# Attention over 3,202 keys: the sums of the probabilities folded by adding transfers instead of a product

## The chip, the core and the metric

The kernel runs on one core of a Trainium2 chip. The metric is the device time of one execution in microseconds, lower is better. The engines named below are PE (TensorE), ACT (ScalarE), DVE (VectorE), POOL (GpSimd) and SP (SyncE, which here only issues transfers).

## What is computed

A cross-attention of 4,096 queries over 3,202 keys with 16 heads of 32, a projection and a residual, then a layer of eight experts of which each token takes two. The change touches only the softmax's denominator, the sum over keys.

```python
def _L0_xattn_ref(queries, keys, values, Wq, bq, Wk, bk, Wv, bv, Wo, bo):
    q = (queries @ Wq + bq).reshape(B, L, H, E)
    k = (keys @ Wk + bk).reshape(B, S, H, E)
    v = (values @ Wv + bv).reshape(B, S, H, E)
    scale = 1.0 / sqrt(E)
    scores = jnp.einsum('blhe,bshe->bhls', q, k)
    A = jax.nn.softmax(scale * scores, axis=-1)
    out = jnp.einsum('bhls,bshd->blhd', A, v)
    out = out.transpose(0, 2, 1, 3).reshape(B, L, H * E)
    return out @ Wo + bo
...
    x = x + _L0_xattn_ref(_layernorm(x, axis=-1), ctx_1024, ctx_1024, ...)
    x = x + _L0_ffn_ref(_layernorm(x, axis=-1), ...)
```

## The kernel before

Three stages follow each other: projections of keys, values and queries (to 278 us), the attention (to about 1,935 us), then routing and experts. The change is in the second.

The attention runs in 32 rounds, `it` 0 to 31: four groups of four heads (HG = 4), and in each eight blocks of 512 queries. A round goes through 25 tiles `t` of 128 keys. The 3,202 keys leave two over; they are **the rest**, which is computed for all four heads in one step of its own, on 72 partitions (the same eight rows three times, for high and low parts), at the place REST_TILE of the round.

For each tile PE makes the scores of four heads (12 products of 32 rows, float32 taken as high and low parts), ACT takes the exponential in two instructions, the first head and the other three, into one of P_RING = 9 slots of `probs` (128 keys x 4 heads x 512 queries), and PE weighs the values with it. PE is two tiles ahead with its scores. A slot may be written again, nine tiles on, when PE has weighed it and when it has been added up.

The adding is split. Of 25 tiles DVE adds 21, alternately into `even_sums` (two buffers, by round) and `odd_sums`: 19 adds of 128x2048 in a round, called k = 0 to 18 here; the first two each add two tiles. The tiles PILED = 4, 9, 14, 19 are added by transfers into `pile`, issued by GpSimd: the first a plain copy (`pile_up(it, 0)`), the others adding transfers (`accum_op`), each waiting for the landing of the one before. At the round's end DVE merges `odd_sums` and `pile` into `even_sums` (two instructions, each waiting for the end of its predecessor).

What is left is a sum over the 128 partitions. PE makes it in the next round, at the rest's place: a product of `rest_split` with ones (line 1322) and one of `even_sums` with ones (line 1300), which also spreads the sum over the 32 rows of each head. ACT copies it from PSUM to `recip`; a transfer stores four rows to DRAM, another loads them as 128x16; DVE inverts (INVERT_AT, after add 5), and two more steps store the inverses and broadcast them to `recip`. DVE multiplies the results `o_sb` with them (NORMALISE_AT, after add 9), and SP stores. ACT had fetched the results from PSUM in between the two exponentials of tile 1. The rest's probabilities must be split into a high and a low part before PE can weigh them (tile 21): ACT copies them to `rest_split`, and DVE subtracts, ahead of add 8.

The order on each engine is the order in which the code is written; semaphores with counts join them. Transfers issued by GpSimd run in one queue, those by SP in another. The last round's sums are made by PE after the loop.

## Time and profile before

| | us |
|---|---|
| median of 3 runs | 2379.47 |
| lowest, highest | 2377.31, 2384.11 |
| the profiled execution | 2381.51 |
| its span, first to last instruction | 2379.7 |
| PE, DVE, ACT, POOL busy in the span | 96%, 85%, 78%, 21% |
| granted clock of PE, mean | 0.981 of 2.4 GHz |

The profile is of one execution. A line of a timeline gives start, duration, engine, line of the code, operation, output<-inputs and shape; in brackets how long the engine was idle before it and what ended that. PE, ACT and DVE overlap an instruction's end with the next one's beginning, so pitches (start to start) say what a row of instructions costs, and durations a little more. A product of float32 that the program writes once stands twice in PE's rows.

### The profile page before, as it was taken

What the parts mean: (1) busy time and instruction counts of PE and PEld (TensorE: products, weight loads), DVE (VectorE), ACT (ScalarE), POOL (GpSimd) and SP (SyncE); (2) the same over time, 40 slices, a digit from 0 to 9 for tenths busy, and PEclk for the clock granted to TensorE, in tenths of its full rate; (3) what the DMA queues carried; (4) which work ended last, traced back from release to release, by engine and by line L of the source; (5) the groups of instructions that cost most, each with busy time, mean ns of one, the idle gap of its engine ahead of it and who ended that gap; (6) DMA issues with size and microseconds to landing.
All of it is one profiled execution on the core that took longest, in us unless ns stands there. A gap on an engine that the chain in (4) does not pass through costs nothing. (4 is left out here: it accounts for less than half of the span.)

```text
span 2379.7 us, 49163 instructions
## 1 busy us (share of the span) xinstructions
PE 2275.9 (96%) x19632; PEld 1097.8 (46%) x19632; DVE 2018.2 (85%) x1866; ACT 1855.5 (78%) x2155; POOL 508.8 (21%) x631
## 2 busy tenths in 40 slices
PE   8999699999999999999999999999999999789898
PEld 7878533333333333333333333333333357578786
DVE  4358489999999999999999999999999988867565
ACT  3223299999999999999999999999999956534332
POOL 2213211311111111111111111111111113146664
PEclk9999899999999999999999999999999999889999
DMA  7436564345464455557444434644544467634463
GB/s 267 168 135 213 179 168 108 90 110 114 112 178 108 110 128 134 132 133 199 108 112 112 117 90 128 155 114 108 117 97 101 101 175 266 205 106 141 147 205 120
DMA packets 140924, 333.70 MB, mean 140 GB/s; under 512 B 28918, under 2 KB 61654, under 8 KB 123548
## 3 DMA queue, kind: packets, MB, share of 16 engines
q0 software_dynamic: 43008, 193.75, 33.8%
q1 hardware_dynamic: 95356, 129.20, 16.6%
q10 hardware_dynamic: 2336, 7.60, 0.9%
q8 instruction: 160, 2.62, 0.5%
q14 instruction: 64, 0.52, 0.1%
HBM read 131.16 MB, written 82.78 MB: 90 GB/s over the span
## 5 line engine op out<-in xcount | busy, mean ns | idle before, releaser
L1133 ACT ACTIVATE probs<-psum 128x1536 f32<-128x1536 f32 x800 | 1164.7, 1456 | 0.0
L1300 PE MATMUL psum<-probs,v_st 128*32 128x512 f32 x6400 | 853.2, 605 | 0.2 <-ACT probs L1133 0.2
L1251 PE MATMUL psum<-q_st,k_st 32*128 32x512 f32 x9600 | 779.1, 425 | 43.2 <-ACT probs L1130 27.4
L1251 PEld LDWEIGHTS psum<-q_st,k_st 32*128 32x128 f32 x9600 | 402.2, 183 | 745.5 <-ACT probs L1130 431.0
L1207 DVE TENSOR_TENSOR even_sums<-even_sums,probs 128x2048 f32<-128x2048 f32 x288 | 658.6, 2287 | 75.6 <-ACT probs L1133 74.6
L1207 DVE TENSOR_TENSOR odd_sums<-odd_sums,probs 128x2048 f32<-128x2048 f32 x256 | 588.4, 2299 | 3.1 <-ACT probs L1133 3.1
L1130 ACT ACTIVATE probs<-psum 128x512 f32<-128x512 f32 x800 | 481.0, 601 | 40.1 <-PE psum L1251 32.4
L1300 PEld LDWEIGHTS psum<-probs,v_st 128*32 128x32 f32 x6400 | 126.1, 108 | 289.0 <-issue 278.8
L2087 PE MATMUL psum<-we_hi,wo 128*128 x624 | 219.1, 412 | 7.6 <-ACT wo L1926 4.4
L948 POOL DMA_DIRECT2D pile<-probs x96 | 85.2, 888 | 495.4 <-DMA pile<-probs 308.2
L2087 PEld LDWEIGHTS psum<-we_hi,wo 128*128 128x128 f32 x624 | 119.7, 192 | 34.4 <-issue 8.7
L1919 ACT ACTIVATE shared_rows<-hold 128x512 f32<-128x512 f32 x78 | 63.5, 815 | 91.0 <-DMA hold<-token_rows,whole 49.0
L2087 PE MATMUL psum<-we_lo,wo 128*128 x312 | 125.0, 401 | 0.0
L945 POOL DMA_DIRECT2D pile<-probs x32 | 18.0, 564 | 495.0 <-ACT probs L1133 470.8
L1926 ACT ACTIVATE wo<-psum 128x512 fp32r<-128x512 f32 x78 | 46.3, 593 | 89.3 <-PE psum L2073 73.6
L345 POOL TENSOR_TENSOR squares<-o_hi 128x512 fp32r<-128x512 f32 (+1 forms) x60 | 60.6, 1018 | 207.0 <-ACT o_hi L383 120.1
L763 PE MATMUL psum<-wo,q_st 128*128 128x512 f32 x384 | 96.4, 400 | 0.0
L383 ACT ACTIVATE o_hi<-psum,bk_col 128x512 fp32r<-128x512 f32 (+1 forms) x28 | 17.4, 642 | 91.7 <-PE psum L593 91.7
L1207 DVE TENSOR_TENSOR even_sums<-probs 128x2048 f32<-128x2048 f32 x32 | 73.1, 2285 | 12.6 <-ACT probs L1133 12.6
L1978 DVE TENSOR_TENSOR wo<-psum,wo 128x512 fp32r<-128x512 f32 x78 | 53.9, 691 | 35.2 <-ACT wo L1926 26.9
L763 PEld LDWEIGHTS psum<-wo,q_st 128*128 128x128 f32 x384 | 73.5, 191 | 16.6
L1212 DVE TENSOR_TENSOR even_sums<-even_sums,odd_sums 128x2048 f32<-128x2048 f32 x32 | 74.3, 2322 | 1.1
(229 smaller groups left out, 2262.8 us busy)
## 6 DMA issues: line engine op xcount, KB each, us to landing
pile<-probs POOLq DMA_DIRECT2D x128, 1024.0 KB, 7.5
token_rows<-rows SPq DMA_DIRECT2D x8, 1028.0 KB, 6.7
xn<-in_x SPq DMA_DIRECT2D x16, 512.0 KB, 6.5
qh_scratch<-o_hi SPq DMA_DIRECT2D x8, 1024.0 KB, 4.5
ql_scratch<-o_lo SPq DMA_DIRECT2D x8, 1024.0 KB, 7.5
q_st<-qh_scratch SPq DMA_DIRECT2D x32, 256.0 KB, 4.4
q_st<-ql_scratch SPq DMA_DIRECT2D x32, 256.0 KB, 5.1
token_rows<-in_x SPq DMA_DIRECT2D x8, 1024.0 KB, 7.6
```

The source lines that it names most:

```text
L345: pool.tensor_tensor(squares[:, j, 0:w], h, h, ALU.mult).then_inc(squared, 1)
L763: mm = pe.matmul(psum[:, bank, :], A[:, j, :], W[:, j, :], start=False, stop=t == len(terms) - 1)
L948: pool.dma_start(out=pile[:], in_=probs[:, p_slot(it, t)], accum_op=ALU.add).then_inc(piled, 16)
L1130: act.activation(probs[:, p, 0, :], psum[:, FIRST_BANK, :], ACT.Exp, bias=-WIDEST, scale=SCALE).then_inc(first_done, 1)
L1133: act.activation(probs[:, p, 1:HG, :], psum[:, bank(t, 1):bank(t, 1) + HG - 1, :], ACT.Exp, bias=-WIDEST, scale=SCALE).then_inc(exp_done, 1)
L1207: nc.vector.tensor_tensor(into[:], a, probs[:, p_slot(it, t)], ALU.add).then_inc(added, 1)
L1212: nc.vector.tensor_tensor(total[:], total[:], odd_sums[:], ALU.add).then_inc(added, 1)
L1251: return nc.tensor.matmul(psum[:, bank(t, h), :], k_st[rows, part, t * P:(t + 1) * P], q_st[it % 2][rows, of, :], start=start, stop=stop)
L1300: mm = nc.tensor.matmul(psum[h * DH:(h + 1) * DH, bank, :], lhs(h), rhs(h), start=start, stop=stop)
L1919: act.activation(xs[s % 2], r[:, 0:D], ACT.Identity, bias=r[:, SHIFT_AT:SHIFT_AT + 1], scale=r[:, RSTD_AT:RSTD_AT + 1]).then_inc(xs_done, 1)
L1978: dve.tensor_tensor(x_lo[s % 2], psum[:, T_BANK + s % 2, :].rearrange("p (k n) -> p k n", k=KT), x_hi[s % 2].bitcast(F32), ALU.subtract).t ...
L2087: mm = pe.matmul(psum[:, OUT_BANKS[s % 4], :], A[s % 2][:, k, :], W[:, k, ds(e, 1), :].rearrange("p o n -> p (o n)"), start=t == 0, stop=t ...
```

## The change

REST_TILE moves from 5 to 2: scores and exponential of the rest stand in a round's third place, ahead of tile 2. ACT fetches the results of the round before right ahead of that exponential, no longer inside tile 1. Splitting the rest moves to GpSimd: a `tensor_copy` of 72x512 and a `tensor_tensor` of 8x512.

The sum over partitions is no product any more, but for the last round's. GpSimd issues three adding transfers that fold `even_sums` onto its first 64, 32 and 16 partitions, a store of these 16 rows to DRAM beside the rest's two rows, and four loads that gather the 18 rows of each head as 128 partitions x 18 x 16 (`spread`). DVE reduces over the 18 and inverts, now after add 11, and normalises after add 15. The inverse's round trip through DRAM is as before; GpSimd issues it between the piles of tiles 14 and 19.

```diff
-REST_TILE = 5
+REST_TILE = 2
+FOLDED, REST_KEYS = 16, 2
 PILED = (4, 9, 14, 19)
-REST_LOW_AT, REST_V_AT, REST_AT = 8, 13, 21
-INVERT_AT, NORMALISE_AT = 5, 9
+REST_V_AT, REST_AT = 13, 21
+INVERT_AT, NORMALISE_AT = 11, 15
 WO_AFTER, REST_AFTER = 3, 5
-FETCH_TILE = 1
...
-    spread = sb("spread", [P, CH // DH], F32)
-    spread_inv = sb("spread_inv", [P, CH // DH], F32)
-    sum_d, inv_d = (dram(name, [HG, CH], F32) for name in ("sum_scratch", "inv_scratch"))
+    fold_d = [dram(f"fold_scratch{b}", [FOLDED + REST_KEYS, HG, CH], F32) for b in range(2)]
+    inv_d = dram("inv_scratch", [HG, CH], F32)
     sums_ready = sem("sums_ready")
-    sums_copied = sem("sums_copied")
-    bounced = sem("bounced")
+    sums_moved = sem("sums_moved")
+    rest_stored = sem("rest_stored")
     sums_spread = sem("sums_spread")
...
+MOVES = {P // 2: 0, P // 4: 1, P // 8: 2, "store": 3, "inverse": 4}
+
+
+def moved(it, what):
+
+    return 16 * (it * len(MOVES) + MOVES[what] + 1)
+
+
+def fold_sums(pool, a, it, total, rows):
+    if 2 * rows in MOVES:
+        pool.wait_ge(a["sums_moved"], moved(it, 2 * rows))
+    pool.dma_start(out=total[0:rows], in_=total[rows:2 * rows], accum_op=ALU.add).then_inc(a["sums_moved"], 16)
+
+
+def store_folded(pool, a, it, total):
+    pool.wait_ge(a["sums_moved"], moved(it, FOLDED))
+    pool.dma_start(a["fold_d"][it % 2][0:FOLDED], total[0:FOLDED]).then_inc(a["sums_moved"], 16)
+
+
+def store_rest(pool, a, it, rest_probs, REST, LAST):
+    rows = a["fold_d"][it % 2][FOLDED:].rearrange("x h q -> h x q")
+    for h in range(HG):
+        pool.dma_start(rows[h], rest_probs[h * LAST:(h + 1) * LAST, :]).then_inc(a["rest_stored"], 16)
+
+
 def spread_sums(pool, a, it):
-    pool.wait_ge(a["sums_copied"], it + 1)
-    pool.dma_start(a["sum_d"], a["recip"][0:P:DH, :]).then_inc(a["bounced"], 16)
-    pool.wait_ge(a["bounced"], it * 32 + 16)
-    pool.dma_start(a["spread"][:], a["sum_d"].rearrange("h (p f) -> (h p) f", p=DH)).then_inc(a["sums_spread"], 16)
+    pool.wait_ge(a["sums_moved"], moved(it, "store"))
+    pool.wait_ge(a["rest_stored"], 16 * HG * (it + 1))
+    for h in range(HG):
+        pool.dma_start(a["spread"][h * DH:(h + 1) * DH], a["fold_d"][it % 2][:, h, :].rearrange("r (p f) -> p r f", p=DH)).then_inc(a["sums_spread"], 16)
+
+
+def store_inverses(pool, a, it):
+    pool.wait_ge(a["inverted"], 2 * (it + 1))
+    pool.dma_start(a["inv_d"].rearrange("h (p f) -> (h p) f", p=DH), a["spread_inv"][:]).then_inc(a["sums_moved"], 16)
 
 
 def broadcast_inverses(pool, a, it):
-    pool.wait_ge(a["inverted"], it + 1)
-    pool.dma_start(a["inv_d"].rearrange("h (p f) -> (h p) f", p=DH), a["spread_inv"][:]).then_inc(a["bounced"], 16)
-    pool.wait_ge(a["bounced"], it * 32 + 32)
+    pool.wait_ge(a["sums_moved"], moved(it, "inverse"))
+    if it > 0:
+        pool.wait_ge(a["o_final"], it)
     for h in range(HG):
         pool.dma_start(a["recip"][h * DH:(h + 1) * DH, :], a["inv_d"][h:h + 1, :].to_broadcast([DH, CH])).then_inc(a["inv_in"], 16)
 
 
 def invert_sums(dve, a, it):
-    dve.wait_ge(a["sums_spread"], it * 16 + 16)
-    dve.reciprocal(a["spread_inv"][:], a["spread"][:]).then_inc(a["inverted"], 1)
+    dve.wait_ge(a["sums_spread"], (it + 1) * (16 * HG))
+    dve.tensor_reduce(a["spread_sum"][:], a["spread"][:].rearrange("p r f -> p f r"), AX.X, ALU.add).then_inc(a["inverted"], 1)
+    dve.wait_ge(a["inverted"], 2 * it + 1)
+    dve.reciprocal(a["spread_inv"][:], a["spread_sum"][:]).then_inc(a["inverted"], 1)
 
 
...
+                def split_rest(it):
+                    pool.wait_ge(exp_done, it * STEPS + REST_TILE + 1)
+                    store_rest(pool, results, it, rest_probs, REST, LAST)
+                    if it > 0:
+                        pool.wait_ge(pv_done, (it - 1) * NT + REST_AT + 1)
+                    pool.tensor_copy(rest_split[:], rest_probs[:]).then_inc(rest_high, 1)
+                    pool.wait_ge(rest_high, it + 1)
+                    pool.tensor_tensor(rest_split[DH:DH + REST, :], rest_probs[DH:DH + REST, :],
+                                       rest_split[DH:DH + REST, :].bitcast(F32), ALU.subtract).then_inc(rest_ready, 1)
+                    pool.wait_ge(rest_ready, it + 1)
+
                 for it in range(NIT):
+                    total = even_sums[(it - 1) % 2]
+                    if it > 0:
+                        pool.wait_ge(added, it * adds)
+                        fold_sums(pool, results, it - 1, total, P // 2)
+                    split_rest(it)
                     pile_up(it, 0)
                     if it > 0:
-                        spread_sums(pool, results, it - 1)
-                        broadcast_inverses(pool, results, it - 1)
+                        fold_sums(pool, results, it - 1, total, P // 4)
+                        fold_sums(pool, results, it - 1, total, P // 8)
+                        store_folded(pool, results, it - 1, total)
                     else:
                         pool.wait_ge(wo_hi_ready, 1)
                         pool.tensor_tensor(wo_lo, wo_raw[:], wo_hi.bitcast(F32), ALU.subtract).then_inc(wo_lo_ready, 1)
-                    for i in range(1, len(PILED)):
-                        pile_up(it, i)
+                    pile_up(it, 1)
+                    if it > 0:
+                        spread_sums(pool, results, it - 1)
+                    pile_up(it, 2)
+                    if it > 0:
+                        store_inverses(pool, results, it - 1)
+                        broadcast_inverses(pool, results, it - 1)
+                    pile_up(it, 3)
...
-                def copy_sums(it):
-                    act.wait_ge(sums_ready, it + 1)
-                    if it > 0:
-                        act.wait_ge(o_final, it)
-                    act.activation(recip, psum[:, SUM_BANK, :], ACT.Copy).then_inc(sums_copied, 1)
-
...
                     act.wait_ge(s_ready, it * STEPS + REST_TILE + 1)
                     if it > 0:
                         act.wait_ge(rest_ready, it)
+                        act.wait_ge(rest_stored, 16 * HG * it)
                     act.activation(rest_probs[:], psum[0:REST_ROWS, REST_BANK, :], ACT.Exp, bias=-WIDEST, scale=SCALE).then_inc(exp_done, 1)
-                    act.wait_ge(exp_done, it * STEPS + REST_TILE + 1)
-                    if it > 0:
-                        act.wait_ge(rest_used, it)
-                    act.activation(rest_split[:], rest_probs[:], ACT.Copy).then_inc(rest_high, 1)
...
                         if t == REST_TILE:
+                            if it > 0:
+                                fetch(it - 1)
                             rest(it)
-                            if it > 0:
-                                copy_sums(it - 1)
                         if t == FIRST_HIGH_TILE and it == NIT - 1:
...
-                        if t == FETCH_TILE and it > 0:
-                            fetch(it - 1)
...
                     if k == 0 and it > 1:
-                        dve.wait_ge(sums_ready, it - 1)
+                        dve.wait_ge(sums_moved, moved(it - 2, "store"))
...
-                        if k == REST_LOW_AT:
-                            dve.wait_ge(rest_high, it + 1)
-                            dve.tensor_tensor(rest_split[DH:DH + REST, :], rest_probs[DH:DH + REST, :],
-                                              rest_split[DH:DH + REST, :].bitcast(F32), ALU.subtract).then_inc(rest_ready, 1)
...
                         if t == REST_TILE:
                             rest_scores(it, shifted)
-                            if it > 0:
-                                sum_probs(it - 1, SUM_BANK)
```

The instructions as the program issues them, GpSimd in the second round, before (lines 945 and 948 are the piles; `shared_rows` holds `recip` and the results):

```order
L945 DMA pile<-probs 128x2048
L777 DMA sum_scratch<-shared_rows 4x512
L779 DMA spread<-sum_scratch 128x16
L784 DMA inv_scratch<-spread_inv 128x16
L787 DMA shared_rows<-inv_scratch 32x512 x4
L948 DMA pile<-probs 128x2048 x3
```

and with the change (976 and 979 are the piles now, CAST is the `tensor_copy`):

```order
L785 DMA even_sums<-even_sums 64x2048
L796 DMA fold_scratch<-rest_probs 2x512 x4
L986 CAST rest_split<-rest_probs 72x512
L988 TENSOR_TENSOR rest_split<-rest_probs,rest_split 8x512
L976 DMA pile<-probs 128x2048
L785 DMA even_sums<-even_sums 32x2048
L785 DMA even_sums<-even_sums 16x2048
L790 DMA fold_scratch<-even_sums 16x2048
L979 DMA pile<-probs 128x2048
L803 DMA spread<-fold_scratch 32x18x16 x4
L979 DMA pile<-probs 128x2048
L808 DMA inv_scratch<-spread_inv 128x16
```

The first pile of a round now stands behind a fold, four stores and two computing instructions; the second, third and fourth each behind a part of the sums' way.

PE at the rest's place in the second round, before (in the branch for wide scores, which has the products with `shift_ones` and `rest_shift` in addition; the runs take the other):

```order
L1285 MATMUL psum<-q_st,rest_k 72x512 x3
L1288 MATMUL psum<-q_st,rest_shift 72x512
L1322 MATMUL psum<-rest_split,rest_ones 128x512
L1300 MATMUL psum<-even_sums,ones 32x512 x4
L1251 MATMUL psum<-q_st,k_st 128x512 x12
```

and with the change:

```order
L1340 MATMUL psum<-probs,v_st 32x512 x4
L1325 MATMUL psum<-q_st,rest_k 72x512 x3
L1328 MATMUL psum<-q_st,rest_shift 72x512
L1291 MATMUL psum<-q_st,k_st 128x512 x12
L1315 MATMUL psum<-q_st,shift_ones 128x512 x4
```

The two products of sums are gone, and the scores of the next tile stand right behind the rest's.

## Rows read from the trace of the kernel before

**Rows 1.** The page, part 1: busy us and share of each engine.
```profile
PE 2275.9 (96%) x19632; PEld 1097.8 (46%) x19632; DVE 2018.2 (85%) x1866; ACT 1855.5 (78%) x2155; POOL 508.8 (21%) x631
```

**Rows 2.** Timeline of PE, turn of one round: start, us, line, operation [idle before].
```profile
1016.96 0.98 PE L1251 MATMUL psum<-q_st,k_st 32*128 32x512 f32 x12 [0.65 <-ACT probs L1130]
...
1020.79 0.92 PE L1285 MATMUL psum<-q_st,rest_k 128*72 128x512 f32 x3
1021.54 0.39 PE L1322 MATMUL psum<-rest_split,rest_ones 72*128 72x512 f32 x1
1021.87 1.06 PE L1300 MATMUL psum<-even_sums,ones 128*32 128x512 f32 x8
1022.86 0.97 PE L1251 MATMUL psum<-q_st,k_st 32*128 32x512 f32 x12
...
1024.75 0.97 PE L1251 MATMUL psum<-q_st,k_st 32*128 32x512 f32 x12
```

**Rows 3.** Timeline of ACT, same round and the next.
```profile
1014.48 0.60 ACT L1083 ACTIVATE shared_rows<-psum 128x512 f32<-128x512 f32 x1 [0.41 <-PE psum L1300]
...
1021.74 0.61 ACT L1096 ACTIVATE rest_probs<-psum 72x512 f32<-72x512 f32 x1
1022.39 0.63 ACT L1100 ACTIVATE rest_split<-rest_probs 72x512 fp32r<-72x512 f32 x1
1023.00 0.60 ACT L1089 ACTIVATE shared_rows<-psum 128x512 f32<-128x512 f32 x1
...
1072.35 0.61 ACT L1096 ACTIVATE rest_probs<-psum 72x512 f32<-72x512 f32 x1
```

**Rows 4.** Timeline of DVE, same round.
```profile
1019.44 2.29 DVE L1207 TENSOR_TENSOR even_sums<-probs 128x2048 f32<-128x2048 f32 x1
...
1025.85 2.29 DVE L1207 TENSOR_TENSOR even_sums<-even_sums,probs 128x2048 f32<-128x2048 f32 x1 [1.93 <-ACT probs L1133]
...
1034.67 0.24 DVE L792 RECIPROCAL spread_inv<-spread 128x16 f32<-128x16 f32 x1
1035.32 2.29 DVE L1207 TENSOR_TENSOR even_sums<-even_sums,probs 128x2048 f32<-128x2048 f32 x1 [0.41 <-ACT probs L1133]
...
1039.84 0.68 DVE L1221 TENSOR_TENSOR rest_split<-rest_probs,rest_split 8x512 fp32r<-8x512 f32 x1
...
1070.04 2.28 DVE L1207 TENSOR_TENSOR even_sums<-probs 128x2048 f32<-128x2048 f32 x1
```

**Rows 5.** Timeline of DVE, projections.
```profile
28.65 0.68 DVE L473 TENSOR_REDUCE k_norms<-psum 128x512 f32 x1
```

**Rows 6.** Instructions of line 345 (GpSimd, projections): ns least/median/most.
```profile
L345 POOL TENSOR_TENSOR squares<-o_hi x60: 403/1042/1248, 21.3 to 274.7; 128x512 fp32r<-128x512 f32 x56, 128x130 fp32r<-128x130 f32 x4
```

**Rows 7.** Timeline of DVE, first and third round.
```profile
318.71 5.87 DVE L1207 TENSOR_TENSOR odd_sums<-odd_sums,probs 128x2048 f32<-128x2048 f32 x1 [0.72 <-ACT probs L1133]
...
451.94 2.29 DVE L1207 TENSOR_TENSOR even_sums<-even_sums,probs 128x2048 f32<-128x2048 f32 x1
454.26 3.26 DVE L1212 TENSOR_TENSOR even_sums<-even_sums,odd_sums 128x2048 f32<-128x2048 f32 x1
```

**Rows 8.** Timeline of GpSimd, the same two places.
```profile
316.94 5.50 POOL L957 TENSOR_TENSOR wo<-even_sums,wo 128x2048 fp32r<-128x2048 f32 x1 [7.29 <-DMA pile<-probs]
...
444.59 10.78 POOL L962 TENSOR_TENSOR bo_pair<-bo_raw,bo_pair 32x512 fp32r<-32x512 f32 x1
```

**Rows 9.** What line 945 issues (tile 4, plain 1 MB): landing.
```profile
DMA to landing us min/median/max: 4.4/4.6/8.0
```

**Rows 10.** What line 948 issues (adding 1 MB): landing.
```profile
DMA to landing us min/median/max: 6.9/7.8/11.7
```

**Rows 11.** View of DMA issues: us to landing of 8 KB transfers on GpSimd's queue.
```profile
sum_scratch<-shared_rows POOLq DMA_DIRECT2D x31, 8.0 KB, 3.1
spread<-sum_scratch POOLq DMA_DIRECT2D x31, 8.0 KB, 2.0
```

**Rows 12.** Stretches of 5 us: busy of each engine, PEclk, DMA share.
```profile
1930.00:1935.00 5.00, 1.93 (x8) 0.20 (x8) 3.26 (x3) 0.00 (x0) 0.00 (x0) 0.77 0.00 0
```

More of the change, by code:

```diff
@@ L812, in attention @@
     O_BANK, LAST_SUM_BANK = ATTENDED_BANK, FIRST_BANK
-    results = g["last"]
     TPC = CH // P
@@ L819, in sb @@
             return sb0(name, shape, dt, mem)
+        results = {**g["last"], "spread": sb("spread", [P, FOLDED + LAST, CH // DH], F32),
+                   "spread_sum": sb("spread_sum", [P, CH // DH], F32), "spread_inv": sb("spread_inv", [P, CH // DH], F32)}
         k_st = sb("k_st", [P, 2, S], F32R)
@@ L856, in attention @@
         rest_ready = sem("rest_ready")
-        rest_used = sem("rest_used")
         rest_k_in = sem("rest_k_in")
@@ L879, in attention @@
         added = sem("added")
-        sums_ready, sums_copied, o_final, o_left = (results[n] for n in "sums_ready sums_copied o_final o_left".split())
+        sums_ready, o_final, o_left, sums_moved, rest_stored = (
+            results[n] for n in "sums_ready o_final o_left sums_moved rest_stored".split())
         small_in, wo_in, wo_hi_ready, wo_lo_ready, o_stored = (
@@ L889, in load_k @@
                 sp.dma_start(k_st[:, part:part + 1, first:first + n].bitcast(F32), src[:, ds(j, 1), first:first + n]).then_inc(count, 16)
-        assert STEPS % 2 == 0 and LAST == 2
+        assert STEPS % 2 == 0 and LAST == REST_KEYS
         def place(t):
@@ L901, in attention @@
         REST_BANK = SETS[REST_TILE % 2]
-        SUM_BANK = REST_BANK + 1
         summed = [t for t in range(NT) if t not in PILED]
@@ L962, in _ @@
                         pool.tensor_tensor(bo_pair[DH:2 * DH, 0:D], bo_raw[DH:2 * DH, :], bo_pair[DH:2 * DH, 0:D].bitcast(F32), ALU.subtract).then_inc(wo_lo_ready, 1)
+                        pool.wait_ge(wo_lo_ready, 2)
             @block.sync
@@ L1320, in sum_probs @@
                 def sum_probs(it, bank):
-                    nc.tensor.matmul(psum[:, bank, :], rest_ones[:], rest_split[:], start=True, stop=False).then_inc(rest_used, 1)
+                    nc.tensor.matmul(psum[:, bank, :], rest_ones[:], rest_split[:], start=True, stop=False)
                     pe.wait_ge(added, (it + 1) * adds)
@@ L1697, in _ @@
                 split_attended_low(dve, g, 2)
-                dve.wait_ge(results["sums_ready"], LAST + 1)
+                dve.wait_ge(results["sums_ready"], 1)
                 step(dve.reciprocal(results["recip"], psum_sums))
```

## Prediction

> **What bounds the kernel now.** Read the page's busy shares first [rows 1]: PE 96%, DVE 85%, ACT 78%, POOL 21%. A share is only a hint, so the next view is the timeline of one round of the attention, a round being one of the 32 repetitions of (4 heads, 512 queries) over 25 tiles of keys. On PE the scores of one tile and those of the next start 1.89 us apart (1022.86 and 1024.75, [rows 2]), and PE has no gap in between. A whole round, from one rest exponential on ACT to the next, takes 1072.35 - 1021.74 = 50.6 us [rows 3]. 32 of them are 1,620 of the 2,380 us. 25 tiles are 47.3 of a round. The remainder is what stands once in a round: the three rest-score products 0.75, the product of the rest's sums 0.33, the sums of `even_sums` 0.99 (differences of starts in [rows 2]), and a stall of 0.65 after the turn of the round, where ACT had to wait for the last product before it could fetch the results [rows 2, 3]; 0.6 is left for the weighing of the rest and what is smaller. So PE bounds a round.
>
> DVE is close behind, and the reader should see how close. Its adds follow each other every 2.20 us and take 2.29 each: they overlap, so DVE shows no gap at all between them. In one round, add 0 to add 0, it is idle 1.93 us before the third add and 0.41 before the seventh [rows 4], and for practically nothing else: 2.3 of 50.6 us.
>
> **What the change takes away.** From PE the two products of sums, 0.33 + 0.99 = 1.32 us a round. From ACT the split (0.61) and the copy of the sums (0.60) [rows 3]. Fetching at the third tile rather than inside the second one no longer makes ACT wait. Its price is that the scores of tile 2 now stand right behind the rest's and need tile 1's exponentials, about 0.3 us where 0.65 was lost. PE's round becomes 50.6 - 1.32 - 0.35 = 48.9 us. ACT, which follows PE through the round, sheds as much, so it doesn't take the bound over. If nothing else ended later this would be 1.7 x 31 = 53 us less.
>
> From DVE the low part of the rest goes (0.68 and the 0.1 gap ahead of it [rows 4]). Added are a reduction of 288 values a partition and a wait between it and the reciprocal. A reduction of 512 took 0.68 [rows 5], so I take 0.45, and 0.8 for reduction, wait and reciprocal where the reciprocal alone had 0.24 [rows 4]; no range wider than 0.2 to 1.0. DVE's work in a round is then 48.3 - 0.8 + 0.55 = 48.05 us. Its reserve shrinks from 2.3 to 0.85 us, and the 1.93 gap, made by the long turn of the round, closes almost wholly.
>
> **What it adds on GpSimd.** Per round: one adding transfer of 512 KB; four small stores; a CAST of 72x512 and a TENSOR_TENSOR of 8x512; the plain copy of tile 4; adding transfers of 256 and 128 KB; a store; then, each between two of the old piles, four gathers of 64-byte pieces, and the inverse's round trip. This queue is strictly in order, so all that stands behind the CAST waits for it. First of all, the copy of tile 4, whose slot in the ring of nine ACT needs for tile 13. Now it lands 4.6 us after its issue [rows 9], and tile 13 comes eight tiles, 15 us, after tile 5.
>
> The two computing instructions are the crux. Alone a 128x512 TENSOR_TENSOR on GpSimd takes 1.04 us [rows 6], and I take that for both (bounds 0.4 to 1.3; there is no CAST on it in this trace). But beside DVE's adds the trace shows something else, twice. In the first round GpSimd started a long one (5.50 us) at 316.94, and the add that DVE started at 318.71 took 5.87 in place of 2.29: it ended 2.1 after GpSimd had finished [rows 7, 8]. In the third round GpSimd started a 32x512 one at 444.59 with DVE in its row of adds. It took 10.78 us [rows 8]. The adds went on undisturbed up to the one at 451.94, and only the merge at 454.26 took 3.26, 0.97 too long [rows 7]. That merge is the one DVE instruction that has to wait for its predecessor's end. So the instruction needed 1 us of work, and waited 9.7 us, past four boundaries between adds, until DVE really stopped. **Two DVE inputs in SBUF and a reading GpSimd instruction exclude each other, and a row of overlapping adds never lets go.**
>
> The Trainium skill (SBUF — State Buffer, section "Who interferes with whom") states the same exclusion: a DVE instruction with two SBUF inputs contends with a GpSimd one that reads SBUF, and the second blocks until the first finishes. Taken literally, GpSimd would get in at the next end of an add; by the row of 10.78 us it did not. That reading is the third rival below.
>
> **The round as it will run.** Count from DVE's add 0, at which the merged sums are complete. GpSimd issues the 512 KB transfer (about 0.9) and four stores (4 x 0.55) and asks for the CAST at 3.1. DVE is in its adds. Its old gap at the third add is 0.2 or closed, and once DVE is later than ACT by half a microsecond the one at the seventh add is closed too. So both GpSimd instructions wait, and with them the copy of tile 4. ACT runs into tile 13, whose slot is not free. DVE adds tiles up to 12 (adds 0 to 8) and then has nothing to add; there GpSimd gets in. From there everything is a chain that ends at the next add 0:
> - nine adds, 9 x 2.20 = 19.8;
> - the two GpSimd instructions, 2 x 1.04 = 2.1;
> - the copy of tile 4, 4.6 to landing [rows 9], with the 256 KB behind it in the same queue, plus 1.5: a small transfer lands in about 2 to 3.1 [rows 11] and an adding one of 1 MB in 7.8 [rows 10], so some 5.8 us a MB; together 6.1;
> - the 128 KB, by the same line 2.8; the issue of the store 0.6;
> - the pile of tile 9, issued before the gathers and ahead of them in the queue: 7.8 [rows 10];
> - the gathers behind it: 1.5. The bound below is 0.3, as for the 8 KB gather now; above I allow 5 for 2,304 pieces of 64 bytes;
> - reduction and reciprocal 0.8, then seven adds 15.4, the normalisation 0.7 and about 1 of waiting for its inverses (a round trip behind the pile of tile 14), two merges 4.6.
>
> The sum is 63.2 us. It is self-consistent: DVE, held up at its reduction, starts the next round later than ACT, so the early gaps stay closed. Against 50.6 it is 12.6 more, in 30 rounds (the first has nothing to fold, the second still runs ahead) 378 us. In ten rounds SP reloads keys or fills the table, and landings reach 11.7 in place of 7.8 [rows 10]; now that they are in the chain this costs up to 3.9 x 10 = 39, of which I take half. From the profiled execution's 2381.5: 2381.5 + 378 + 20 = **2780 us**. (That execution is 2.0 above the median of the three runs, which is nothing here.)
>
> PE stands still some 11 us at tile 13 in this picture. Where PE stood still for 3.1 of 5 us, the granted clock of that stretch was 0.77 [rows 12]: it had fallen to 1.2 GHz at the stand's end. So PE will restart at half its speed. At 3.7 us a tile for two or three tiles it falls some 4 us behind, but DVE is at that time waiting for its gathers anyway: I put it at nothing, and at 4 us x 30 = 120 if that cover fails.
>
> **The rivals.**
> *Gaps are caught earlier.* If DVE is ahead of ACT at the third and the seventh add, the CAST enters at about 4 and the other at about 15, the copy of tile 4 is issued 8 us sooner, and the same chain gives 57 us a round: + 6.4 x 31 = 198, 2580. For it: in the first rounds DVE does run ahead. Against it: its reserve of 0.85 is less than the 2.1 that the two instructions cost it, and the gathers still land too late.
> *GpSimd is let in at the next boundary.* Then the two only cost their own time, DVE's round is 48.05 + 2.1 = 50.15, against 50.6: 2381.5 - 14 = 2367, from 2355 to 2400, about the same as before. Against it stands the 10.78.
> *Nothing is held up*, since 72 and 8 partitions or a CAST behave otherwise: PE's 48.9 decides, 2381.5 - 53 = 2329. This is the side of faster, and the point from which it decides is that both GpSimd instructions end within about 8 us of the CAST's start; only then does the copy of tile 4 land before tile 13. For it: the piles of tiles 9 and 14 land no later than now. Against it: both collisions in this trace, in either order.
> *Worse*: 5 us of gathers and PE's slow clock uncovered: 70 us a round, 2960 and more.
>
> **How the numbers follow.** The forecast, both instructions let in only where DVE starves, 0.68. Earlier gaps 0.13. Next boundary 0.07. Nothing held up 0.09. Worse than 2960 0.03. The range 2480 to 2960 takes in the forecast's own bounds (gathers 0.3 to 5, instructions 0.4 to 1.3, landings 6.9 to 11.7) and the earlier gaps, together 0.8. A difference of 0.3% (7 us) is about what a measurement of this kernel can tell from none. Faster by more: 0.09 and most of the next-boundary case, 0.13; within it 0.04; slower 0.83.
>
> **What would show each step.** Right: the GpSimd instructions on `rest_split` last 10 us or more, not 1; ACT waits for the pile's transfer before tile 13, some 11 us in each round; DVE idles before its tenth add and at its reduction, for the spread; a round of about 63 us. PE's products of sums are gone but for the last, and PE's share falls to about 80%. Wrong: `rest_split` instructions of 1 to 3 us and a round of 49 to 50.5 us. If they are long but the round is under 60, the order of gaps is what I have wrong; if over 66, it is a landing, the gathers' first of all.

## The result

The changed kernel took 2505.92 us (median of four runs, 2503.86 to 2508.36) against 2379.05 for the kernel before (2377.31 to 2384.11): a ratio of 1.053, with a 95% interval of 1.051 to 1.055. It is slower by 127 us. The direction is the one forecast, and the time lies in the range (2480 to 2960), but near its lower edge: the forecast was +400. A round of the attention, add 0 to add 0, now takes 55.0 us in the mean of 31 (median 54.5), where 63.2 was forecast and the mean was 50.9 before (median 50.6, as in [rows 3]). 31 times 4.06 us are 126 of the 127, so the whole loss lies in the attention's rounds.

### The profile page after: what moved, and what is told of

It is laid out like the page before. It is cut to its first block and busy times, and to the rows that moved or that the text cites. A ratio compares the mean times of both kernels' runs of the same rounds, so it can differ in the third digit from the quotient of the medians.

```text
span 2505.6 us, 48921 instructions
## 1 busy us (share of the span) xinstructions
PE 2294.5 (92%) x19353; PEld 1102.5 (44%) x19353; DVE 2059.2 (82%) x1865; ACT 1828.1 (73%) x2092; POOL 864.6 (35%) x1009
## 3 DMA queue, kind: packets, MB, share of 16 engines
q10 hardware_dynamic: 2336, 7.60, 0.9%
## 5 line engine op out<-in xcount | busy, mean ns | idle before, releaser
L1291 PE MATMUL psum<-q_st,k_st 32*128 32x512 f32 x9600 | 807.2, 438 | 151.2 <-ACT probs L1176 130.7
L1340 PE MATMUL psum<-probs,v_st 128*32 128x512 f32 x6400 | 879.6, 623 | 0.2 <-ACT probs L1177 0.2
L1291 PEld LDWEIGHTS psum<-q_st,k_st 32*128 32x128 f32 x9600 | 415.8, 190 | 868.2 <-issue 414.4
L1176 ACT ACTIVATE probs<-psum 128x512 f32<-128x512 f32 x800 | 478.2, 598 | 206.7 <-DMA pile<-probs 134.1
L1251 DVE TENSOR_TENSOR odd_sums<-odd_sums,probs 128x2048 f32<-128x2048 f32 x256 | 620.7, 2425 | 1.9 <-ACT probs L1177 1.9
L785 POOL DMA_DIRECT2D even_sums<-even_sums x93 | 77.0, 828 | 596.0 <-DVE even_sums L1259 408.3
L979 POOL DMA_DIRECT2D pile<-probs x96 | 90.7, 944 | 128.6 <-DMA pile<-probs 112.3
L816 POOL DMA_DIRECT2D shared_rows<-inv_scratch x124 | 61.8, 505 | 209.9 <-DMA inv_scratch<-spread_inv 207.8
L803 POOL DMA_DIRECT2D spread<-fold_scratch x124 | 84.5, 689 | 64.6 <-DMA fold_scratch<-even_sums 59.9
L988 POOL TENSOR_TENSOR rest_split<-rest_probs,rest_split 8x512 fp32r<-8x512 f32 x32 | 102.3, 3196 | 2.7
L2016 DVE TENSOR_TENSOR wo<-psum,wo 128x512 fp32r<-128x512 f32 x78 | 53.9, 691 | 50.5 <-ACT wo L1964 50.5
L821 DVE TENSOR_REDUCE spread_sum<-spread 128x16 f32<-128x288 f32 x31 | 20.3, 655 | 86.4 <-DMA spread<-fold_scratch 86.4
```

The costliest lines, as they stand in the source:

```text
L785: pool.dma_start(out=total[0:rows], in_=total[rows:2 * rows], accum_op=ALU.add).then_inc(a["sums_moved"], 16)
L803: pool.dma_start(a["spread"][h * DH:(h + 1) * DH], a["fold_d"][it % 2][:, h, :].rearrange("r (p f) -> p r f", p=DH)).then_inc(a["sums_spre ...
L979: pool.dma_start(out=pile[:], in_=probs[:, p_slot(it, t)], accum_op=ALU.add).then_inc(piled, 16)
L988: pool.tensor_tensor(rest_split[DH:DH + REST, :], rest_probs[DH:DH + REST, :], rest_split[DH:DH + REST, :].bitcast(F32), ALU.subtract).the ...
L1176: act.activation(probs[:, p, 0, :], psum[:, FIRST_BANK, :], ACT.Exp, bias=-WIDEST, scale=SCALE).then_inc(first_done, 1)
L1251: nc.vector.tensor_tensor(into[:], a, probs[:, p_slot(it, t)], ALU.add).then_inc(added, 1)
```

## The profile after

The page's busy shares, the counterpart of [rows 1]:

```profile
PE 2294.5 (92%) x19353; PEld 1102.5 (44%) x19353; DVE 2059.2 (82%) x1865; ACT 1828.1 (73%) x2092; POOL 864.6 (35%) x1009
```

No engine has become the bound; all three stand still more than before. The view of waits says for whom (engine, tile and line, what it waited for: us in all, times, longest):

```profile
POOL shared_rows L816 <- DMA inv_scratch<-spread_inv: 207.8, 31, 7.7
...
ACT probs L1176 <- DMA pile<-probs: 134.1, 33, 7.6
PE psum L1291 <- ACT probs L1176: 130.7, 35, 7.4
...
DVE spread_sum L821 <- DMA spread<-fold_scratch: 86.4, 31, 6.7
...
DVE shared_rows L830 <- DMA shared_rows<-inv_scratch: 45.4, 30, 4.0
DVE even_sums L1251 <- ACT probs L1177: 44.4, 27, 11.7
```

GpSimd waits 6.7 us a round for the landing of the inverses' store, which stands in the queue behind the pile of tile 14; what of that reaches DVE is the wait at the normalisation (line 830). ACT's 4.1 us for a pile (134.1 over 33) is a wait for the pile of tile 9, and PE's is its echo. DVE waits at the reduction (line 821) for the gathered sums, and in the adds for ACT; 11.7 of those 44.4 are its start. One round shows where these waits stand. Add 0 of this round is at 963.14 and that of the next at 1017.14, 54.0 us on. GpSimd's part first:

```profile
963.52 0.83 POOL L785 DMA_DIRECT2D even_sums<-even_sums  x1 [13.13 <-DVE even_sums L1259]
964.07 2.30 POOL L796 DMA_DIRECT2D fold_scratch<-rest_probs  x4
966.42 1.67 POOL L986 CAST rest_split<-rest_probs 72x512 fp32r<-72x512 f32 x1
968.18 3.19 POOL L988 TENSOR_TENSOR rest_split<-rest_probs,rest_split 8x512 fp32r<-8x512 f32 x1
971.67 0.58 POOL L976 DMA_DIRECT2D pile<-probs  x1 [0.30 <-POOL rest_split L988]
972.24 0.87 POOL L785 DMA_DIRECT2D even_sums<-even_sums  x1
979.15 0.78 POOL L785 DMA_DIRECT2D even_sums<-even_sums  x1 [6.03 <-DMA even_sums<-even_sums]
983.57 0.52 POOL L790 DMA_DIRECT2D fold_scratch<-even_sums  x1 [3.64 <-DMA even_sums<-even_sums]
984.08 0.93 POOL L979 DMA_DIRECT2D pile<-probs  x1
987.04 2.73 POOL L803 DMA_DIRECT2D spread<-fold_scratch  x4 [2.03 <-DMA fold_scratch<-even_sums]
```

The two instructions on `rest_split` took 1.67 and 3.19 us, not 10. Both got in at the next boundary between two adds. Tile 4's copy (971.67) is issued 8.5 us after add 0; the forecast had 21.9. DVE and ACT:

```profile
967.54 2.70 DVE L1251 TENSOR_TENSOR even_sums<-even_sums,probs 128x2048 f32<-128x2048 f32 x1
970.16 3.36 DVE L1251 TENSOR_TENSOR odd_sums<-odd_sums,probs 128x2048 f32<-128x2048 f32 x1
...
992.85 0.60 ACT L1176 ACTIVATE probs<-psum 128x512 f32<-128x512 f32 x1 [2.55 <-DMA pile<-probs]
...
993.57 0.65 DVE L821 TENSOR_REDUCE spread_sum<-spread 128x16 f32<-128x288 f32 x1 [2.43 <-DMA spread<-fold_scratch]
994.25 0.25 DVE L823 RECIPROCAL spread_inv<-spread_sum 128x16 f32<-128x16 f32 x1
...
999.93 2.29 DVE L1251 TENSOR_TENSOR even_sums<-even_sums,probs 128x2048 f32<-128x2048 f32 x1 [1.08 <-ACT probs L1177]
...
1005.27 0.69 DVE L830 TENSOR_TENSOR shared_rows<-shared_rows 128x512 f32<-128x512 f32 x1 [0.85 <-DMA shared_rows<-inv_scratch]
```

The two adds that the GpSimd instructions push aside take 0.4 and 1.1 us more. ACT's stop is not at tile 13 but at tile 18, whose slot holds tile 9, until its pile has landed; it is there in all 31 rounds, 4.2 us in the mean. DVE waits at the reduction (2.43) for the gathered sums, then for ACT (1.08), then at the normalisation (0.85). That is 4.4 us idle and 1.5 us of pushing in a round.

The views of the lines on GpSimd (duration: ns least/median/most):

```profile
L986 POOL CAST rest_split<-rest_probs x32: 607/1668/1956, 303.0 to 2010.8; 72x512 fp32r<-72x512 f32 x32
L988 POOL TENSOR_TENSOR rest_split<-rest_probs,rest_split x32: 3187/3196/3207, 303.7 to 2012.3; 8x512 fp32r<-8x512 f32 x32
```

In none of 32 rounds did either last 4 us. The view of DMA issues (times, size, median us to landing) prices the new transfers and shows the store of the inverses:

```profile
even_sums<-even_sums POOLq DMA_DIRECT2D x31, 512.0 KB, 5.2
...
even_sums<-even_sums POOLq DMA_DIRECT2D x31, 256.0 KB, 6.5
...
spread<-fold_scratch POOLq DMA_DIRECT2D x124, 36.0 KB, 5.0
even_sums<-even_sums POOLq DMA_DIRECT2D x31, 128.0 KB, 4.1
...
inv_scratch<-spread_inv POOLq DMA_DIRECT2D x31, 8.0 KB, 6.8
```

## Experiments: what the change costs

Two theories stood after the result. **A**: the loss is one chain, from the merge over the folds, the pile of tile 9 and the gathers to the reduction, and the GpSimd instructions matter because they stand at its head. **B**: the folds are too long by themselves (contention, adding transfers), wherever the instructions stand. The later experiments ask what of the change is worth anything.

**The rest split on ACT and DVE again.**

```diff
-                    pool.tensor_copy(rest_split[:], rest_probs[:]).then_inc(rest_high, 1)
...
-                    pool.tensor_tensor(rest_split[DH:DH + REST, :], rest_probs[DH:DH + REST, :],
...
+                    act.activation(rest_split[:], rest_probs[:], ACT.Copy).then_inc(rest_high, 1)
...
+                        if k == 8:
+                            dve.wait_ge(rest_high, it + 1)
+                            dve.tensor_tensor(rest_split[DH:DH + REST, :], rest_probs[DH:DH + REST, :],
...
```

> The changed kernel with the rest split as before: ACT copies right after the rest's exponential (0.61 us), DVE subtracts ahead of add 8 (0.68). All else is as changed. Theory A, the two GpSimd instructions hold up the queue: in the changed kernel the copy of tile 4 is issued 8.5 us after add 0; without them it is 3.2, so everything behind is 5.3 us sooner, the gathers land 25 us after add 0, before DVE asks for them (27), and PE and DVE decide again: 49.2 us a round in place of 54.0, 2379 - 31 x 1.4 = 2336 us. Theory B, the added transfers are what costs (folds and gathers share the engines of the piles): the round stays over 52.5, 2440 us or more.

2386.57 us (10 runs), ratio to before 1.0017 (1.0008 to 1.0027). So the two instructions, where they stand, carry 119 of the 127 us, though they work for only 1.7 us (0.6 and 1.0, the shortest of their kind). The 2336 was missed too: the median round is 50.7 us. The reduction waits in only three rounds (16.5 us in all), but the normalisation waits as it did in the changed kernel (46.9 us in all, 45.4 there). One of its longer waits:

```profile
1010.01 0.69 DVE L830 TENSOR_TENSOR shared_rows<-shared_rows 128x512 f32<-128x512 f32 x1 [2.25 <-DMA shared_rows<-inv_scratch]
```

**The same two instructions on GpSimd, but behind the third pile.**

```diff
                     store_rest(pool, results, it, rest_probs, REST, LAST)
+
+                def compute_rest(it):
...
                     pool.tensor_copy(rest_split[:], rest_probs[:]).then_inc(rest_high, 1)
...
                     pile_up(it, 2)
+                    compute_rest(it)
```

> The changed kernel with GpSimd's two instructions on the rest moved from ahead of the first pile to behind the third; the four small stores stay. Theory A, queue order: as e1, but DVE loses the 1.5 us that the two instructions took from its adds in the changed kernel: a round of about 49.6 to 50.3, 2350 to 2370 us. Theory C, DVE's port: the two cost their time wherever they stand, and where DVE is late (no add waits for a tile) they wait 10 us as the 32x512 one did in the kernel before; then the inverses and the last pile are late too and the round is 55 us or more, over 2500 us.

2387.75 us, ratio 1.0024 (1.0012 to 1.0036): the same as with ACT and DVE, and outside both expectations (the normalisation's wait is left here too, 36.2 us in all). It isn't GpSimd's share of work that costs, but its place at the head of the queue. What remains of the pushing is about what ACT and DVE paid for the split.

**Without the folds** (the three adding transfers left out, so the denominators lack 112 of 128 partitions; GpSimd's instructions stay at the head).

```diff
-MOVES = {P // 2: 0, P // 4: 1, P // 8: 2, "store": 3, "inverse": 4}
+MOVES = {"store": 0, "inverse": 1}
...
-                        fold_sums(pool, results, it - 1, total, P // 2)
...
-                        fold_sums(pool, results, it - 1, total, P // 4)
-                        fold_sums(pool, results, it - 1, total, P // 8)
```

> The changed kernel without its three adding fold transfers: 16 partitions of the unfolded sums are stored, so the denominators leave out the other 112 partitions. GpSimd's two instructions stay ahead of the first pile. Theory A: the copy of tile 4 is still issued some 7.5 us after add 0, but the pile of tile 9 goes out about 11 us sooner and is no longer late; DVE decides with 48.05 + 1.5: a round of 49.6 to 50.2, about 2355 us. Theory B, it is the load on the transfer engines other than the folds (gathers of 64 bytes): still 52 or more a round.

2343.01 us (one run), a round of 49.4, a little under what theory A gave. With the head of the chain as it is and its middle gone, no wait is left at the reduction. Together with the first two: either part of the chain taken out is enough, its head or its folds, as A has it. B would have left the first two slow.

**Tile 4's copy ahead of the two instructions.**

```diff
                     store_rest(pool, results, it, rest_probs, REST, LAST)
+
+                def compute_rest(it):
...
                     pile_up(it, 0)
+                    compute_rest(it)
```

> The changed kernel with the plain copy of tile 4 ahead of GpSimd's two instructions on the rest in place of behind them; folds, gathers and the other piles stay behind both. Theory A (the changed kernel is held up by what stands between the two instructions and the end of the gathers, that is by the second pile and the gathers, and the copy of tile 4 is not late): nothing or less than 1 us a round is won, 2480 to 2510 us. Theory of the prediction (tile 4's copy is the one ACT waits for): 3 us a round or more is won, under 2420.

2444.05 us (one run). Neither number was right. 62 us are saved, about 2.0 a round. The copy of tile 4 goes out 5.5 us sooner, and ACT still stops at tile 18 in all 31 rounds, so that copy is not what it waits for. What got shorter is the landing of the 256 KB fold, which no longer stands right behind a copy of 1 MB in the queue: it was issued at 1000.30 and its successor at 1005.12, where the changed kernel needed from 972.24 to 979.15.

```profile
1000.30 0.84 POOL L785 DMA_DIRECT2D even_sums<-even_sums  x1 [0.31 <-POOL rest_split L990]
1005.12 0.78 POOL L785 DMA_DIRECT2D even_sums<-even_sums  x1 [3.99 <-DMA even_sums<-even_sums]
```

Its median landing in the view of DMA issues is 4.6 us, where the changed kernel has 6.5:

```profile
even_sums<-even_sums POOLq DMA_DIRECT2D x31, 256.0 KB, 4.6
```

**The normalisation two adds later** (on the kernel of the first experiment, and on that of the second).

```diff
-INVERT_AT, NORMALISE_AT = 11, 15
+INVERT_AT, NORMALISE_AT = 11, 17
```

> e1 (rest split by ACT and DVE) with DVE's normalisation after add 17 in place of 15, 4.4 us later. In e1 DVE waits 2.25 us in each round for the inverses, whose store lands 7.0 us after its issue because the pile of tile 14 is ahead of it in the queue. If that wait is what keeps e1 at 50.6 to 50.9 us a round, it goes, and DVE's 48.9 and PE's 48.9 decide: 49.2 a round, 2330 to 2345 us. If DVE's wait only hides another (ACT waiting for piles, 0.5 us at three places), it stays above 2370.

> The change with both GpSimd instructions behind the third pile and the normalisation after add 17 in place of add 15. Theory: what was left in the variant without the later normalisation (2387.75) was its wait of 1.60 us a round for the inverses, so 25 to 45 us go: 2345 to 2362, level with the variant that splits on ScalarE and VectorE and normalises after add 17 (2355.5). Rival: DVE's own time is the bound there, with 1.1 to 1.5 us a round lost to the shared access in place of 0.7 for the subtraction, so the later normalisation gives less than 15 us: 2373 or more.

2355.50 us, ratio 0.9892 (0.9875 to 0.9908), and 2359.65, ratio 0.9894 (0.9877 to 0.9911). Both beat both kernels, by 1% the one before. The second expectation held. The normalisation has no wait left in either. The forecast of the first (2330 to 2345) was too good by 10 to 25 us. The median round of that kernel is 49.3 us, add 0 to add 0, but the eighth, sixteenth and twenty-fourth, in which SP reloads keys, take 54.9, 57.7 and 54.3, and some after them up to 52.4. In the kernel before the same three took 50.6, 51.2 and 51.4, and without the folds 50.2 to 50.5. Over its usual round the three cost 19 us more here, 3 without the folds and 1.4 before. So the folds make the reload costly, some 16 us in those three; by which transfer, no run here separates.

## Experiments: why the forecast's wait did not come

The forecast rested on one row, a GpSimd instruction of 32x512 that took 10.78 us in the middle of DVE's adds [rows 8]. All 64 instructions of the changed kernel took 0.6 to 3.2.

**Idle GpSimd instructions in the kernel before**, two in a round, of four shapes, on scratch tiles.

```diff
+                        if i == 2:
+                            probe(it % 4, 1 + (it > 2))
+                        if i == 3:
+                            probe((it // 4 + it) % 4, 1 + (it > 2))
...
+                        pool.tensor_tensor(probe_out[DH:2 * DH, :], probe_in[DH:2 * DH, :], probe_in[DH:2 * DH, :], ALU.subtract).then_inc(probed, 1)
...
+                        pool.tensor_copy(probe_out[0:72, :], probe_in[0:72, :]).then_inc(probed, 1)
```

> The kernel before with idle instructions added on GpSimd that read and write a scratch tile: one behind the third and one behind the fourth pile of each round, in turn 32x512 TENSOR_TENSOR, 8x512 TENSOR_TENSOR, 72x512 copy, 128x512 TENSOR_TENSOR. DVE is in its row of adds at both. Theory of the prediction (overlapping adds never let go): they last until DVE's next stop, 5 to 14 us each. Theory of the Trainium skill's wording (SBUF - State Buffer, the second waits until the first finishes): each lasts at most 2.3 us of waiting and about 1 of work, and the add behind it is as much longer. Theory D (it depends on the instruction or on the moment): some long, some short, and the trace tells by what.

2391.5 us. The view of their lines (line numbers of this run's kernel; ns least/median/most):

```profile
L962 POOL TENSOR_TENSOR probe_out<-probe_in x16: 1127/2078/2926, 332.5 to 1825.8; 32x512 f32<-32x512 f32 x16
L964 POOL TENSOR_TENSOR probe_out<-probe_in x16: 1031/2252/3212, 386.3 to 1875.3; 8x512 f32<-8x512 f32 x16
L966 POOL COPY probe_out<-probe_in x16: 648/1667/2652, 437.5 to 1925.3; 72x512 f32<-72x512 f32 x16
L968 POOL TENSOR_TENSOR probe_out<-probe_in x16: 1028/1942/4402, 487.8 to 1917.2; 128x512 f32<-128x512 f32 x16
```

63 of 64 waited for no more than one DVE instruction (the 3.2 us are those that asked in the last 0.1 us of an add and waited out the next); 8 partitions cost as much as 128. This is what the Trainium skill states (SBUF — State Buffer, section "Who interferes with whom"): the second of the two instructions waits until the first has finished. The one of 4.40 and the row of 10.78 do not follow it, and had to be explained.

**The kernel before once more, and the lone instruction elsewhere.** First the kernel unchanged; then seven copies of line 962's instruction on scratch tiles, one every fourth round; then line 962 itself in the seventh round in place of the third.

```diff
+                    if it % 4 == 2 and it > 2:
+                        pool.wait_ge(idled, it // 4 + 1)
+                        pool.tensor_tensor(idle_pair[DH:2 * DH, :], idle_raw[DH:2 * DH, :], idle_pair[DH:2 * DH, :].bitcast(F32), ALU.subtract).then_inc(idled, 1)
```

> The kernel before, unchanged, profiled a second time. The question is the one row on which the forecast rested: line 962, 32x512, 10.78 us in the first profile. If waiting until VectorE stops is what this place of the program always gives (the forecast's theory, of this instruction if of no other), it takes 9 to 12 us again. If it was an exception, as one of 64 idle instructions was, it takes 1.0 to 3.2 us. Time 2377 to 2384 in either case.

> The kernel before with the instruction of line 962 left in the third round, and seven copies of it on scratch tiles (same engine, shape, types and in-place form), one behind the last pile of rounds 7, 11, 15, 19, 23, 27 and 31, so that GpSimd computes nothing for some 200 us ahead of each. If it is this rarity that makes the instruction wait for VectorE's stop (the 64 idle instructions came two in a round), the seven take 5 to 11 us each. If waiting at most for the running VectorE instruction is the rule and round three is a place of its own, they take 1.0 to 3.2 us each and line 962 again 10.8.

> The kernel before with the instruction of line 962 in the seventh round in place of the third. If the place in the third round is what is special, it takes 1.0 to 3.2 us there. If it is this instruction, alone after a long time, it takes 5 to 11 us again. The time stays within 0.3% of 2381 either way.

The times were 2381.04, 2378.38 and 2381.89 us. The line of the instruction in the kernel unchanged, then that of the seven copies:

```profile
L962 POOL TENSOR_TENSOR bo_pair<-bo_raw,bo_pair x1: 10796/10796/10796, 444.5 to 444.5; 32x512 fp32r<-32x512 f32 x1
```

```profile
L970 POOL TENSOR_TENSOR idle_pair<-idle_raw,idle_pair x7: 6801/10461/11092, 648.1 to 1866.8; 32x512 fp32r<-32x512 f32 x7
```

In the run with the seven copies line 962 itself took 10.79 us, and in the seventh round it took 10.51. So the row was no exception at all. In this program, behind the last pile, waiting for the end of DVE's row is the usual thing. These runs left it open whether that is so because the instruction is rare.

**Its distance in time varied**, 50, 100 and 150 us.

```diff
+                IDLE_IN = (5, 6, 7, 8, 9, 10, 12, 14, 16, 18, 20, 23, 26, 29)
...
+                    if it in IDLE_IN:
+                        pool.wait_ge(idled, IDLE_IN.index(it) + 2)
+                        pool.tensor_tensor(idle_pair[DH:2 * DH, :], idle_raw[DH:2 * DH, :], idle_pair[DH:2 * DH, :].bitcast(F32), ALU.subtract).then_inc(idled, 1)
```

> The kernel before with the same lone 32x512 instruction on scratch tiles behind the last pile, now at several distances in time: in rounds 6 to 11 each (50 us apart; the first of them 150 us after line 962), in rounds 13, 15, 17, 19, 21 (100 us apart), and in rounds 24, 27, 30 (150 us apart). If the time since GpSimd last computed decides, the 50 us ones take 1.0 to 3.2 us, the 150 us ones 6 to 11, and the 100 us ones show on which side they are. If distance doesn't matter and one instruction a round differs from two for another reason, all take 6 to 11 us.

Both expectations failed (2382.39 us): of the five at 50 us four took 8.7 to 10.9 and one 2.2; of the five at 100 us two took 10.3 and 10.4, the others at most 2.0; of the four at 150 us three took 8.9 to 10.5, one 1.6. Distance in time does not decide. What orders them is how far DVE is behind ACT. In the kernel before, GpSimd asked at 444.59, during the add that had started at 443.13. ACT's second exponential of that add's tile ended at 443.01, 0.12 us before its start:

```profile
441.56 1.45 ACT L1133 ACTIVATE probs<-psum 128x1536 f32<-128x1536 f32 x1
...
443.13 2.29 DVE L1207 TENSOR_TENSOR even_sums<-even_sums,probs 128x2048 f32<-128x2048 f32 x1
```

Read like this for every lone and every idle instruction in all runs on the kernel before (the next one included), the add that is *running* when GpSimd asks had its tile ready 0.1 to 0.5 us before its own start in 20 of the 22 cases in which GpSimd waited past a boundary, and 0.56 us or more in all but three in which it did not. The three, of different runs, asked between 1519 and 1523 us, in the same round. The later adds of a row have a longer distance (0.43 to 1.04 us in that round), and GpSimd was not let in at them either; so it is the distance at the time of asking that orders the cases, not the one at each boundary.

**DVE made 0.7 us later**: one 8x512 instruction on a scratch tile ahead of add 11, all else as in the run before.

```diff
+                        if k == 11:
+                            dve.wait_ge(idled, 2)
+                            dve.tensor_tensor(late_in[DH:DH + 8, :], idle_raw[0:8, :], idle_raw[0:8, :], ALU.subtract)
```

> The kernel of the distances in time, with one more 8x512 instruction on VectorE ahead of add 11 of every round, on a scratch tile. It makes VectorE some 0.7 us later behind ScalarE for the rest of the round: the tile of the next add is ready about 1.1 to 1.5 us before its start where GpSimd asks, in place of 0.4 to 0.8. In the runs so far GpSimd had to wait for the end of the row where this was 0.4 to 0.8 and where the add before had 0.5 or less, and got in at the next boundary where it was over 0.85. If VectorE's lag decides, nearly all 15 lone instructions (line 962's copy and the 14 on scratch) now take 1.0 to 3.2 us. If it is something else in the program of before, most take 8 to 11 us again, as 10 of 15 did.

2384.84 us. The same 14 instructions, without and with it:

```profile
L971 POOL TENSOR_TENSOR idle_pair<-idle_raw,idle_pair x14: 1594/9146/10852, 599.8 to 1822.5; 32x512 fp32r<-32x512 f32 x14
```

```profile
L972 POOL TENSOR_TENSOR idle_pair<-idle_raw,idle_pair x14: 1592/2672/3087, 597.5 to 1823.5; 32x512 fp32r<-32x512 f32 x14
```

All 15 (the copy in the third round among them, 2.79 us) now got in at the next boundary. At add 14, the one running in most of these cases, DVE was now 0.97 us behind its tile in place of 0.11 to 0.16. A shift of DVE by 0.8 us, away from GpSimd's instruction and without touching it, turned 10 us into 3. That making DVE later ends the long wait is shown. That it acts through DVE's distance behind ACT is argued from the order of the cases. By what means it would, and why five of the cases did not follow it (the three, and two of the 22), stays open.

In the changed kernel the instructions stand at the start of a round, right behind the merges, where DVE is well behind ACT. At the CAST of 966.42 the running add had started at 965.34, 1.67 us after its tile was ready. In every round but the first this distance was 1.6 us or more at the CAST. The TENSOR_TENSOR asks during the add that the CAST has pushed; it got in at that add's end in all rounds. In seven of them (the one shown among them) that add had started only 0.03 to 0.46 us after its tile was ready, so the distance alone does not tell when GpSimd is kept out. These seven asked within 0.1 us of another GpSimd instruction's end; whether that matters, no run here tests.

## The prediction, point by point

- **PE bounds a round before, the two sums' products go, 1.7 us saved a round.** Right. The kernel without folds has 49.4, the one with the later normalisation 48.7 to 49.3, against the 48.9 worked out. This gain is real, and the changed kernel hides it.
- **Reduction and reciprocal 0.8.** 0.65 and 0.25, right. DVE's small reserve was read rightly too: 1.5 us of pushing is more than it.
- **Both GpSimd instructions wait until DVE starves.** This is the step that failed, and with it "a row of overlapping adds never lets go". The row had been read rightly, and it repeats (10.80). What was wrong was to carry it to another place. The prediction itself said that DVE would be late behind ACT in the early adds, and took that for a reason why GpSimd would not get in; it is the very state in which the CAST did get in, in each of 31 rounds. From add 0 to the issue of tile 4's copy it was 8.5 us, not nine adds and two instructions (21.9): 13.4 us a round too much. That is more than the whole error of a round (63.2 - 54.0 = 9.2); the folds and a wait, below, give 4.1 back.
- **The chain merge, folds, pile of tile 9, gathers, reduction, seven adds, merges.** Right as a shape, and it is what bounds the round. Measured, add 0 to add 0: 8.5 to the copy, 7.5 to the landing of the 256 KB fold (forecast 6.1), 4.4 for the 128 KB (2.8), 0.5, then 9.5 from the pile of tile 9 to the gathered sums (7.8 + 1.5 = 9.3), 0.9 for reduction and reciprocal, 20.8 for seven adds, normalisation and merges, and waits of 1.1 and 0.9: together the 54.0. The two folds were undersized by 3.0 us a round. The forecast took them in proportion to their size; measured, 128 KB landed in 4.1 us and 512 KB in 5.2, and 256 KB took 6.5 behind the copy of 1 MB and 4.6 without it.
- **ACT stops at tile 13 for 11 us.** With the copy issued 13 us sooner the stop is at tile 18, for the pile of tile 9: 2.55 us in this round, 4.2 in the mean. PE's share is 92%, not 80%.
- **PE's slow clock put at nothing, since DVE waits for its gathers anyway.** Not quite. DVE's wait ended at 993.57, but PE had stood still behind ACT's stop, and from 993.5 to 995.2 its granted clock was 0.50, which is 1.2 GHz: the scores took 1.65 us in place of 0.97. ACT waited 0.50 and 0.73 us for PE, and DVE then 1.08 us for ACT. At this place DVE waited in 25 rounds, 31.5 us in all, between the 0 and the 120 of the forecast's two cases. The windows of 5 us (PEclk is the third number from the end):

```profile
985.00:990.00 5.00, 5.00 (x60) 1.82 (x52) 5.00 (x3) 5.00 (x6) 2.75 (x5) 1.00 0.95 185
990.00:995.00 5.00, 2.62 (x24) 1.06 (x20) 2.54 (x4) 2.24 (x3) 1.14 (x2) 0.83 0.49 87
995.00:1000.00 5.00, 5.00 (x48) 1.51 (x48) 3.92 (x3) 3.98 (x5) 0.37 (x1) 0.82 0.93 185
```

- **The rivals.** "Let in at the next boundary" had the mechanism right and its time (2367) wrong: it counted only the instructions' own time. Leaving out the chain cost it nothing by the forecast's own terms, which with 8.5 in place of 21.9 at its head give 63.2 - 13.4 = 49.8, under the 50.15 that it has for DVE. It was the folds' 3.0 and the 1.1 behind PE's slow clock that made the chain 54. "Earlier gaps" came nearest in time (2580), but by another mechanism, and with a slip: its copy 8 us sooner would give 63.2 - 8 = 55.2 a round, about 2524, where it wrote 57. That the time fell into the range is luck: with the head as it was, the forecast's own terms give a time level with before, and only these unforeseen 4.1 us a round carried it in. A chance of 0.68 on a rule with a single clean row behind it was too much.

## What to carry to other kernels

Ahead of a queue that runs strictly in order, ask of each instruction what stands behind it and when that is due: here under 2 us of work at the head of GpSimd's queue cost 119 us of 2,500, and the same work in the middle of it cost no more than it did on ACT and DVE. Before a duration is carried from one place of a trace to another, compare the state of both engines there (who follows whom, and by how much), not only shapes and types. And look for the last wait of a round once the first is mended: moving the normalisation by two adds was worth 28 to 31 us with the head of the queue cleared; on the changed kernel itself no run tries it.

## What the runs showed of the hardware

- A GpSimd instruction on SBUF and a DVE add with two SBUF inputs exclude each other, whatever the partitions: the pushed add takes 2.70 in place of 2.28 us for a copy of 72x512 and 3.1 to 3.4 for a subtraction of 8, 32 or 128 rows.
- GpSimd normally gets in at the end of the running add, but waited up to 11 us in 22 cases, in 20 of which the running add had started less than half a microsecond after its tile was ready. Putting 0.7 us of work on DVE removed that. Such a distance did not always keep it out: ten others (three in variants of the kernel before, seven in the changed kernel) asked at such a distance and got in at the next boundary.
- A transfer on GpSimd's queue is late behind a large one: the 8 KB store of the inverses landed in 6.8 us behind an adding transfer of 1 MB, where 8 KB took 2.0 to 3.1 in the kernel before [rows 11]. The 256 KB fold took 6.5 behind a plain copy of 1 MB and 4.6 without it.
- Small adding transfers keep a large fixed part: 128 KB landed in 4.1 us, 256 KB in 4.6 with no large transfer ahead of it, 512 KB in 5.2.
